# Ternary layers of a two-layer transformer as two streams of steps, even and odd blocks, with tiles of their own

## What is computed

```python
# L0 attention: 16 heads of 8 columns, softmax, out projection, residual, layernorm with gamma and beta
# L0 ffn, the "ternary layers" (weights are -1, 0 or 1, each output has a scale):
h = silu(tlin(x, w1_w, w1_s)) * tlin(x, w2_w, w2_s)      # 128 -> 512
h = gelu(tlin(h, h1_w, h1_s), approximate=False)         # 512 -> 512
h = gelu(tlin(h, h2_w, h2_s), approximate=False)         # 512 -> 512
x = x + tlin(h, w3_w, w3_s)                              # 512 -> 128
# L1 attention, gated linear attention, 8 heads of 16 x 16:
h_t = h_{t-1} * exp(g_t)[..., None] + k_t[..., None] * v_t[..., None, :];  o_t = q_t . h_t
# then rms norm of o, gate by silu(x @ Wg), @ Wo
# L1 ffn: a router on the mean of x picks 3 of 8 zones for each batch; z = gelu(x @ Wa[e]) @ Wb[e]
```

## Time and profile before

| what | us |
|---|---|
| runs before: lowest, median, highest of 3 | 1196.13, 1200.7, 1201.81 |
| the profiled execution, its time | 1197.4 |
| its span, first to last instruction | 1195.6 |
| TensorE, VectorE, ScalarE, POOL busy over the span | 1047.1, 677.9, 833.4, 378.3 |
| busiest groups: exponentials L975, scans L1332, POOL products L937 | 474.3, 205.4, 179.6 |

### The profile page before, as it was taken

How to read it: one execution, slowest core, us unless ns; L and a number is a source line. 1 busy time by engine, 2 the same in 40 slices (tenths; PEclk the granted TensorE clock), 3 DMA queues, 4 the chain that set the end, 5 groups by cost and what they waited for, 6 DMA issues and landing times.

```text
span 1195.6 us, 16803 instructions
## 1 busy us (share of the span) xinstructions
PE 1047.1 (88%) x5936; PEld 519.7 (43%) x5970; DVE 677.9 (57%) x1225; ACT 833.4 (70%) x1073; POOL 378.3 (32%) x391
## 2 busy tenths in 40 slices
PE   2899999999999999997877878879787778878898
PEld 1232333333333333334565544546552344455577
DVE  3122434444444434135453899988778999899300
ACT  2699999999999999995546776665365653534531
POOL 1000000101010100001431778877656554855200
PEclk8799999999999999998887998988877999999999
DMA  5754545546363626100000000000002011010020
GB/s 125 119 115 100 104 86 99 97 79 113 72 113 70 120 45 118 38 17 20 1 1 27 1 28 27 1 27 1 24 4 72 8 45 57 22 35 28 13 67 19
DMA packets 101457, 64.60 MB, mean 54 GB/s; under 512 B 62388, under 2 KB 91860, under 8 KB 99284
## 3 DMA queue, kind: packets, MB, share of 16 engines
q1 hardware_dynamic: 101328, 62.98, 25.3%
q10 hardware_dynamic: 24, 0.25, 0.1%
HBM read 45.10 MB, written 17.83 MB: 53 GB/s over the span
## 4 chain that ended last, share of the span: by engine, by line
PE 58%; DVE 20%; ACT 9%; issue 5%; POOL 4%; SPq 2%; DMA 1%; DVEq 0%; another core or an unknown queue 0%; ACTq 0%; POOLq 0%
PE PS L1529 25%; PE PS L1514 14%; DVE R L1332 7%; PE PS L1563 5%; PE PS L1697 4%; DVE R L1323 4%; PE PS L1686 3%; DVE RB L1279 2%; ACT R L1060 2%; PE PS L1458 1%; DVE R L1289 1%; ACT R L1002 1%; DVE R L1285 1%; POOL rs L881 1%; ACT RB L1003 1%
## 5 line engine op out<-in xcount | busy, mean ns | idle before, releaser
L975 ACT ACTIVATE R<-PS 128x1024 f32<-128x1024 f32 x512 | 474.3, 1089 | 60.6 <-PE PS L1514 60.6
L1529 PE MATMUL PS<-R 128*32 128x512 f32 x2048 | 315.3, 610 | 1.2 <-issue 1.2
L1514 PE MATMUL PS<-RA 34*128 34x512 f32 x1024 | 189.6, 448 | 18.7 <-DMA RA<-QD 18.3
L1332 DVE TENSOR_TENSOR_SCAN R<-R 128x512 f32<-128x512 f32 x128 | 205.4, 1605 | 0.0
L1563 PE MATMUL PS<-RB,WR 128*128 128x512 f32 x640 | 186.5, 440 | 20.2 <-ACT RB L990 7.8
L937 POOL TENSOR_TENSOR R<-R 128x512 f32<-128x512 f32 x128 | 179.6, 1405 | 76.0 <-DVE R L1332 70.8
L1514 PEld LDWEIGHTS PS<-RA 34*128 34x128 f32 x1024 | 77.3, 187 | 215.3 <-issue 194.3
L1563 PEld LDWEIGHTS PS<-RB,WR 128*128 128x128 f32 x640 | 129.3, 205 | 58.3 <-issue 14.3
L1529 PEld LDWEIGHTS PS<-R 128*32 128x32 f32 x2048 | 68.1, 108 | 106.3 <-issue 94.6
L895 POOL PARTITION_ALL_REDUCE R<-R x8 | 3.0, 374 | 291.0 <-DVE R L1169 291.0
L911 POOL TENSOR_TENSOR RB<-R,RB 128x512 fp32r<-128x512 f32 x48 | 71.9, 1506 | 66.5 <-ACT RB L990 56.4
(11 more groups left out here) (137 smaller groups left out, 1112.8 us busy)
## 6 DMA issues: line engine op xcount, KB each, us to landing
RA<-QD SPq DMA_DIRECT2D x256, 64.0 KB
QD<-RA SPq DMA_DIRECT2D x128, 64.0 KB, 2.1
RA<-QD SPq DMA_DIRECT2D x64, 128.0 KB
OD<-R SPq DMA_DIRECT2D x128, 32.0 KB, 2.0
R<-OD SPq DMA_DIRECT2D x128, 32.0 KB
VD<-R SPq DMA_DIRECT2D x24, 128.0 KB, 1.8
R<-VD SPq DMA_DIRECT2D x96, 32.0 KB
WP<-in_Wa SPq DMA_DIRECT2D x12, 256.0 KB, 2.8
```

Of the source, the lines that this page charges most:

```text
L975: act.activation(PR[u % 4], bank(2 * s, 1024), ACT.Exp, scale=SC).then_inc(S["exp"], 1)
L1332: dve.tensor_tensor_scan(st, Ac[k], st, CS[:, v:v + 1] if k else 0.0, ALU.mult, ALU.add).then_inc(S["scanned"], 1)
L1514: op = pe.matmul(bank(2 * s + h), exact(KS[k][p:p + 34, gg, 128 * j:128 * j + 128]), exact(QS[k][p:p + 34, gg, :]), start=True, stop=True)
L1529: op = pe.matmul(bank(ob)[c:c + 32, :], VAF[b % 2][:, at:at + 32], PR[u % 4][:, 512 * h:512 * h + 512], start=(j == 0), stop=(j == 7), til ...
```

## The change

Stream `b` becomes two, `b` for blocks 0, 2, 4, 6 and `c` for blocks 1, 3, 5, 7. Each runs its block from end to end: gates, level 1, level 2, `down`, norm, turn, then its next block. Each has two of the four sets of hidden tiles for its own (2 and 3 for `b`, 0 and 1 for `c`) and writes them by turns, so `slot_free` and the list of free sets go. The tile YN goes too: the normed block is written over the block's own TT. Each `parts` is now a step of its own, so that `ORDER`, a new table of 992 letters in place of 892, can put other steps between a gelu and its `lo`.

Three more edits stand at the seam between attention and rest. `ternary_begin` and the splitting of `XT` of blocks 0 and 1 are written into the last attention block's plan (keys 20, 26 and 28, that is in pairs 30 and 31), and there the `hi` copy is VectorE's. `rest_begin` goes on all engines, and TensorE no longer waits for the last exponential before its first gate matmul: it waits for each bank by itself, for the exponential that reads this bank last.

```diff
 ORDER = (
-    "bbbbbabbabbbbbbbbbbbbbbbbbabbbbbbabbbbabbpbbpbpppbpbppbppppbpbsppsbsbbsssbsbsbsssbbbsssspbpbpssbsbss"
+    "abcbbbbcbbcabbcbbbbcbabbbcbbcbbcbbccbbccacbccacbcccpbbccpbppbpcpccbpcppbppcpbpsppssssssbscscbcsbspcp"
...
+                if b == 7:
+                    plan.setdefault(20, []).append(lambda bk: self.add("ternary_begin"))
+                    plan.setdefault(26, []).append(lambda bk: self.split_x(0))
+                    plan.setdefault(28, []).append(lambda bk: self.split_x(1))
...
     def split_x(self, b):
         k = b % 2
...
+        after = [("xt2", b + 1)] + ([self.xp_free[k]] if b >= 2 else [("exp", 480)])
+        self.parts(("x", b), ("xt", b), ("xp", k), False, "ACT" if b >= 2 else "DVE", after)
+
+    def gates(self, b, L):
+        for m in range(4):
...
+            self.add("gate_mm", b, m, ("xp", b % 2), list(self.parts_of["x", b]), ba, bb, g1, g2)
+            self.add("gate", m, L, ba, bb, pa, pb, tanh, g1, self.tile_free[b % 2])
+            yield
+            self.parts(key, ("hl", L, m), ("hl", L, m), True, "ACT", [g2])
+            yield
+        self.xp_free[b % 2] = pb
...
+            self.add("hid_mm", n0, b, m, [("hl", src, k) for k in range(4)],
+                     [list(self.parts_of[before, b, k]) for k in range(4)], bk, hi)
+            self.add("gelu", dst, m, bk, scale, done)
+            yield
+            self.parts_of[key][0] = hi
+            self.parts(key, ("hl", dst, m), ("hl", dst, m), m % 3 == 1, None, [])
+            yield
+
+    def stream_b(self, k):
+
+        A, B = 2 - 2 * k, 3 - 2 * k
+        for b in range(k, NBLK, 2):
+            if b >= 2:
+                self.split_x(b)
                 yield
+            yield from self.gates(b, A)
+            yield from self.level(2, b, A, B, 8)
+            yield from self.level(6, b, B, A, 12)
+            bk = self.take()
...
+            self.stats_shift("X", b, k, e)
+            yield
+            yn = self.scale("YN", "X", b, k)
...
             def ternary_begin():
-                need.wait_ge("exp", 512)
+                for bk in range(6):
+                    emptied[bk] = ("exp", 510 + (bk // 2 + 1) % 3)
```

More of the change, by code:

```diff
@@ L258, in split_x, with level @@
         k = b % 2
-        key = ("x", b)
-        self.parts_of[key] = [None] * 2
-        after = [("xt2", b + 1)] + ([self.xp_free[k]] if self.xp_free[k] else [])
-        self.parts(key, ("xt", b), ("xp", k), False, True, after)
-        return (("xp", k), [key])
-    def level(self, n0, src, scale, first, into, b):
-        L = self.free_slots.pop(0)
-        got = []
-        tiles, keys = src[0], src[1]
-        done = None
+        self.parts_of["x", b] = [None] * 2
+        after = [("xt2", b + 1)] + ([self.xp_free[k]] if b >= 2 else [("exp", 480)])
+        self.parts(("x", b), ("xt", b), ("xp", k), False, "ACT" if b >= 2 else "DVE", after)
+    def gates(self, b, L):
+        for m in range(4):
+            key = (0, b, m)
+            self.parts_of[key] = [None] * 2
+            ba, bb = self.take(), self.take()
+            pa, pb = self.count("gate_ps"), self.count("up_ps")
+            tanh, g1, g2 = self.count("tanh"), self.count("gated"), self.count("gated_up")
+            self.add("gate_mm", b, m, ("xp", b % 2), list(self.parts_of["x", b]), ba, bb, g1, g2)
[4 more added lines that the diff above has]
+        self.xp_free[b % 2] = pb
+    def level(self, n0, b, src, dst, scale):
+        before = {2: 0, 6: 2}[n0]
         for m in range(4):
@@ L272, in level @@
             self.parts_of[key] = [None] * 2
-            if first:
-                ba, bb = self.take(), self.take()
-                evs = list(self.parts_of[keys[0]])
-                pa, pb = self.count("gate_ps"), self.count("up_ps")
-                done = pb
-                self.count("tanh")
-                g1, g2 = self.count("gated"), self.count("gated_up")
-                self.add("gate_mm", b, m, tiles, evs, ba, bb, g1, g2)
-                self.advance()
-                self.add("gate", b, m, L, ba, bb, pa, pb, self.slot_free[L])
-                self.pending.append(lambda key=key, m=m, g2=g2: self.parts(key, ("hl", L, m), ("hl", L, m), True, True, [g2]))
-            else:
-                bk = self.take()
-                evs = [list(self.parts_of[k]) for k in keys]
-                done = self.count("hid_ps")
-                hi = self.count("gelu")
-                self.add("hid_mm", n0, b, m, tiles, evs, bk, hi)
-                self.advance()
-                self.add("gelu", L, m, bk, scale, done, self.slot_free[L])
-                self.parts_of[key][0] = hi
-                self.parts(key, ("hl", L, m), ("hl", L, m), m % 3 == 1, False, [])
@@ L294, in level @@
-            if m == 0 and self.slot_free[L]:
-                self.add("slot_free", self.slot_free[L])
-            got.append(key)
-            yield
-        if first:
-            self.xp_free[first - 1] = done
-        else:
-            src[2](done)
-        def release(e, L=L):
-            self.slot_free[L] = e
-            self.free_slots.append(L)
-        into[:] = [[("hl", L, m) for m in range(4)], got, release]
-    def down(self, b, src):
-        tiles, keys, release = src
-        bk = self.take()
-        t = self.next_temp()
-        done = self.count("down_ps")
-        release(done)
-        scaled = self.count("down_scaled")
-        evs = [list(self.parts_of[k]) for k in keys]
-        e = self.count("x2")
-        self.add("down", b, tiles, evs, bk, t, done, scaled, self.tt_free[t], e)
-        self.tt_free[t] = e
-        self.x2 = e
@@ L937, in state @@
                 pool.tensor_tensor(st, st, Qc[b % 2], ALU.mult).then_inc(S["qh"], 1)
-            does = dict(stats=stats, pads=pads, flag=flag, weights_flag=weights_flag, rest_begin=rest_begin,
-                        slot_free=slot_free, parts=parts, first_c=first_c, state=state, shift=shift, down=down, last_c=last_c)
+            does = dict(stats=stats, pads=pads, flag=flag, weights_flag=weights_flag, parts=parts, first_c=first_c, state=state, shift=shift, down=down, last_c=last_c)
             for name, *at in order:
@@ L1269, in ternary_begin @@
                 dve.tensor_tensor(sB[:, 4:8], sB[:, 4:8], sB[:, 0:4], ALU.mult).then_inc(S["s_scaled"], 1)
-            def slot_free(e):
-                need.wait_ge(*e)
             def parts(src, dst, pooled, copied, after, first):
+                if copied == "DVE":
+                    for e in after:
+                        need.wait_ge(*e)
+                    dve.tensor_copy(part(tile(dst)[:, 0, :]), whole(src)).then_inc(S["hi"], 1)
                 if not pooled:
```

143 lines of the change are left out of this document (41 added, 102 removed).

## The result

The changed kernel takes 1223.0 us in the median of 4 runs (1221.84 to 1224.51), the kernel before 1201.3 in the runs beside them: 1.0183 times as long, 95% interval 1.0139 to 1.0226. So it is slower, clear of the noise; whether by more than 2% isn't told. The forecast was 1186, and faster. The profiled execution has a span of 1221.7 us, 26.1 more than before, and a granted clock of 0.923 (before 0.937).

The account below looks back on a forecast made before the run. One chain's latency bounds the front, VectorE the stretch from first scan to 1112 us. Span 1195.6 - 11.1 (earlier stage end) - 1.8 (tail) = 1182.7, execution 1184.5, put up to 1186; range 1173 to 1204.

Parts of the forecast that it names:

- Seam: Between attention and rest: VectorE waits for block 7's fetch before `divide`, reaching the first gate product at 556.2, 8.2 us later.
- To the first `down` and scan: Front: fewer steps stand ahead, so the first `down` comes 15 us earlier and the first scan 24.5 us earlier, at 638.8.
- clock rival: Front: TensorE idle at the seam runs at its lower clock, costing 22.2 us; scan 661.0, time 1206.7; chance 0.20.
- bound of 646: Sign at the first scan: the forecast would be wrong if it starts after 646 us.
- Behind the first scan: Middle: VectorE work grows 15.5 to 416.0 us, lasting 462.1 at the old ratio less 4; stage ends 11.1 us earlier.
- given back: Middle: TensorE sets the pace, 76 more matmuls cost 20 us, `lo` parts gain nothing; time 1194; chance 0.20.
- More than that: Middle, 800 to 960 us: two streams never waiting for each other gain 14.5 us instead of 4; time 1175; chance 0.15.
- Tail: After the last scan: one `zone_down` step of 2.84 us moved ahead, 1 us counted back; 1.8 us gained.

Follow-up runs that it names:

- experiment 2: Both hidden levels and `down` read a constant tile instead of hidden tiles, in both kernels: changed kernel 1168.4 us, kernel before 1181.2 us.
- before_near: Kernel before with level 2 written right behind level 1, and `down` with its norm and transposes a round earlier: 1210.0 us, 1.0073.
- after_static: Changed kernel with both hidden levels and `down` reading a constant tile instead of hidden tiles: 1168.4 us, 0.9718.
- four deals: Changed kernel with steps of its two streams reordered in the table, four ways, for more work between dependent steps: 1250.8, 1238.6, 1247.2 and 1228.5 us.

## Why the prediction was wrong

**Seam: right.** The write and fetch of the last pair were priced from the nearest rows: reciprocal at 552.1 forecast, 551.67 measured; first gate product 556.2 forecast, 555.67 measured. VectorE's timeline:

```profile
551.67 3.35 DVE L1119 RECIPROCAL R<-R 128x512 f32<-128x512 f32 x1 [7.28 <-DMA R<-OD]
...
555.67 0.68 DVE L1203 SCALAR_TENSOR_TENSOR R<-R,PS 128x512 f32<-128x512 f32 x1
```

**To the first `down` and scan: the mechanism right, 8.6 us short.** The first step of level 1 was complete, and its gelu began, at 573.72 where 569.0 was forecast: 4.7 us late. Ahead of the last gate's `lo` POOL has its part of block 7's norm, for whose statistics it waited 5.02 us; the forecast had not counted this:

```profile
570.01 0.23 POOL L813 TENSOR_SCALAR rs<-mv 128x4 f32<-128x4 f32 x1 [5.02 <-DVE mv L1056]
570.32 1.04 POOL L815 TENSOR_TENSOR rs<-rs,half 128x4 f32<-128x4 f32 x1
571.33 1.26 POOL L839 TENSOR_TENSOR RB<-R,RB 128x512 fp32r<-128x512 f32 x1
...
573.72 0.69 ACT L922 ACTIVATE R<-PS,sB 128x512 f32<-128x512 f32 x1 [5.95 <-PE PS L1482]
```

The 69 products of 512 columns of the two levels were priced at 0.245 us each, 16.9 us, and took 20.6, 0.32 and 0.28 each in the mean:

```profile
572.89 10.16 PE L1482 MATMUL PS<-RB,WR 128*128 128x512 f32 x32 [5.17 <-POOL RB L839]
...
589.21 10.42 PE L1482 MATMUL PS<-RB,WR 128*128 128x512 f32 x37 [4.30 <-DVE RB L1197]
...
599.47 0.78 PE L1482 MATMUL PS<-WR,RB 128*128 128x128 f32 x6
```

The granted clock from 544 to 599 was 0.78 and from 599 to 647 0.75, behind a TensorE that had stood idle for 10.7 us at the seam and then 5.2 and 4.3 us at the two levels; before it was 0.86 and 0.79. The clock rival named this and gave it 22.2 us; in these 69 products it took 3.7. VectorE's first step behind `down` began at 608.20 instead of 597.3, 10.9 us late: 4.7 by POOL, 3.7 in the products, and the rest in `down` itself, which waited 2.2 us for its last `lo` where half a us was counted and then took 5.59 us for 25 of its products. From there to the first scan it took 39.2 us where 41.5 was forecast. The first scan, at 647.39, lies between the forecast's 638.8 and the rival's 661.0, just past the bound of 646 that the prediction had set itself. The Trainium skill ("TensorE: Matmul & The Clock Gate", Part 1) has a throttled engine released by activity, and the trace agrees: behind its idle time each of the two runs of products begins at the lower level (granted clock 0.50, 1.2 of 2.4 GHz) and ends at the upper one (1.00). The means of 0.32 and 0.28 us mix the two.

```profile
573.00:578.00 5.00, 5.00 (x12) 3.94 (x13) 0.69 (x1) 2.65 (x5) 1.28 (x1) 0.50 0.00 0
579.00:583.50 4.50, 4.05 (x18) 3.00 (x16) 1.84 (x3) 2.94 (x5) 0.77 (x1) 1.00 0.00 0
589.30:591.90 2.60, 2.60 (x6) 2.06 (x7) 0.56 (x1) 1.78 (x3) 0.71 (x1) 0.50 0.02 6
592.50:598.50 6.00, 6.00 (x28) 4.92 (x27) 2.13 (x3) 4.63 (x8) 2.96 (x3) 1.00 0.00 0
```

**Behind the first scan: this step failed.** It took the old ratio of time to VectorE work, 448.7 / 400.5 = 1.12, over to the new order and took off 4 us for `lo` parts that no longer stand directly behind their gelu: 462.1 us for 416.0 of work. Between the first and last scan the changed kernel took 488.08 for 412.15, a ratio of 1.18. The work was sized well enough (15.5 us moved in by the forecast, 12.4 measured); the idle time was forecast at 46 us and is 76. The 4 us taken off had the wrong sign too: between 640 and 900 us VectorE's wait for gelus ahead of a `lo` grew from 11.2 to 16.1 us, and its wait for `down`, put at no change, from 9.0 to 17.9. The ratio isn't a property of VectorE but of the order that was changed. In the kernel before, level 2 of the block before, level 1 of the next block, the gates of the next but one and a `down` stand between the two hidden levels of a block; in two streams that run each block from end to end, a level follows its own input after 2.4 us of TensorE work, about the time of its last gelu and `lo` (0.69 + 0.68 + 0.69 us at the least). The constant operands (experiment 2) show that the waits for hidden tiles' parts hold the whole excess, and before_near that the distance between the levels alone makes about half to two thirds of it in a single stream. That it is the distance also in the changed kernel, and not the two blocks in flight, isn't shown: there longer distances gave nothing back.

The rival "given back" had the right place (TensorE sets the pace in the middle, nothing comes of the `lo` parts) but priced it as throughput, 76 matmuls x 0.26 us, instead of as waits. "More than that" assumed two streams that never wait for each other. They don't share tiles, but they share four in-order engines, so a wait in one stops the other. The forecast counted how many steps stood ahead of the first `down`; it should have counted, for every pair of dependent steps, what stands between them.

**Tail: right in size.** 1.8 us less forecast, 2.0 measured; its two terms weren't looked at one by one.

**In sum**, against the forecast span of 1182.7: 8.6 us in the front, and 30.6 in the middle (44.0 more than before where 13.4 were forecast), -0.2 in the tail: 39.0, the span of 1221.7.

**Open.** The rest of the new idle time, some 11 to 15 us, has no experiment of its own; it may be the other two kinds of boundary (the gates to level 1 have 3.7 us between them in place of 7.0, an estimate like those above) or that only two blocks are in flight. The split of `XT`, for which TensorE waits 9.6 us where it didn't before, wasn't tested by itself either. ScalarE's loads of function tables, 54 of 1.28 us each in the stretch where before has 48, are no candidate: they stay in after_static, whose idle time is that of the kernel before. Whether an order of two streams exists that fills its boundaries wasn't settled: four deals by simple rules failed, and each made new waits. More tiles weren't tried either.

## What to carry over

When a change reorders work on in-order engines, list for each pair of dependent steps the work that stands between them, before and after, and compare it with the latency of the hand-over; a busy ratio read from the old order can't be carried over, because that order made it. Test such waits by constant operands in all the dependent places together: taken away singly they partly stood in for each other here (-8, -1 and -17 us, all three together -55). And a low granted clock beside many short waits may be their consequence: it rose from 0.88 to 0.91 in the middle when the waits were taken away, and filling the idle time raised it as far and gave nothing.

## What the runs showed of the hardware

The front's clock was low though TensorE was busy most of the time: 0.75 from 599 to 647 us with TensorE busy 38.98 of 48.40 us, and in the kernel before 0.79 with 45.37 of 57.30, nearly the same share. A fetch over DRAM, whose four DMAs were issued from 547.60 on, as the timeline shows, had landed at 551.67, 1.6 us behind the last issue:

```profile
547.60 2.45 SPq L739 DMA_DIRECT2D R<-OD  x4
```

And a single late part can hold every engine: the wait of 4.2 us on TensorE that ended at 713.2 us was followed by the ends of waits of 5.65 us on ScalarE (714.1), 1.85 on VectorE (714.8) and 5.75 on POOL (717.5).
